# Sixteen sequences of attention and coupling on one core: the coupling's last half added inside the next attention, exp's table loaded behind the last gelu, VectorE's twists behind its maxima, and the side stages on other beats

## The reference

```
left = layernorm(x)[..., :128]                  # attention, 16 heads of 8
q, k, v = left @ Wq.T, left @ Wk.T, left @ Wv.T
att = softmax(q k^T / 4);   y = (att v) @ Wo.T + bo
x = x + layernorm(y)

out = layernorm(x)                              # coupling, 3 cycles
gf = sigmoid(gelu-net of the mean over tokens)
for _ in range(3):
    tf = sigmoid(gelu(gelu(gelu(out @ w1 + b1) @ w2 + b2) @ w3 + b3) @ w4 + b4)
    out = out + (0.1 + 2 * range * (0.7*gf + 0.3*tf - 0.5)) * twist(out)
x = x + layernorm(out)
```

## Time and profile before

| what | value |
|---|---|
| time, median of 3 runs | 3841.51 us (3839.16 to 3843.34) |
| the profiled execution's own time | 3838.75 us |
| its span, first to last instruction | 3836.9 us |
| mean granted TensorE clock | 0.951 of full |
| busy: PE, DVE, ACT, POOL | 92%, 79%, 78%, 24% of the span |
| a full iteration, first exp to first exp | 229.7 to 231.9 us |

### The profile page before, as it was taken

The page is one execution under the profiler, slowest core; times in us unless marked ns, Lnnn a source line. Parts: engine busy times, 40 slices in busy tenths (PEclk is TensorE's granted clock), DMA queues, the critical chain, the costliest instruction groups (busy, mean ns, idle before and its releaser), DMA issues.

```text
span 3836.9 us, 56226 instructions
## 1 busy us (share of the span) xinstructions
PE 3521.5 (92%) x20096; PEld 1037.1 (27%) x20096; DVE 3022.6 (79%) x5740; ACT 2989.7 (78%) x4014; POOL 904.9 (24%) x1258
## 2 busy tenths in 40 slices
PE   3998999999999999989999999999999999999996
PEld 1222232323223232232322223232232322323232
DVE  3997879788797887879788797887879788797832
ACT  2766969788796978869788796878869788796975
POOL 3002040411405023050311404023050320404033
PEclk7997999999999999999999999999999999999998
DMA  3201112021211202112021211202112021111011
GB/s 66 37 21 38 31 30 28 22 49 21 47 22 34 42 16 52 27 41 28 14 55 23 45 23 34 41 17 49 30 41 28 12 55 25 31 26 34 2 34 22
DMA packets 48405, 123.69 MB, mean 32 GB/s; under 512 B 13568, under 2 KB 14976, under 8 KB 40064
## 3 DMA queue, kind: packets, MB, share of 16 engines
q1 hardware_dynamic: 44960, 101.74, 13.3%
q0 software_dynamic: 2304, 16.78, 2.4%
q10 hardware_dynamic: 864, 1.57, 0.3%
HBM read 34.61 MB, written 33.55 MB: 18 GB/s over the span
## 4 chain that ended last, share of the span: by engine, by line
PE 66%; ACT 11%; DVE 9%; POOL 7%; issue 5%; DMA 1%; SPq 0%; ACTq 0%; POOLq 0%; DVEq 0%
PE heads_ps L416 22%; PE ring_ps L378 13%; PE scoresT_ps L401 9%; DVE max_parts L819 8%; PE scoresT_ps L514 7%; ACT p_sb L603 3%; PE scoresT_ps L519 3%; ACT x_in L616 2%; PE scoresT_ps L525 2%; POOL rstd L977 2%; PE scoresT_ps L522 2%; PE ring_ps L445 2%; ACT headsT L612 1%; ACT y_sb L616 1%; POOL rest L998 1%
## 5 line engine op out<-in xcount | busy, mean ns | idle before, releaser
L819 DVE TENSOR_REDUCE max_parts<-ring_ps 128x1 f32<-128x512 f32 x3782 | 2399.7, 684 | 331.9 <-PE ring_ps L378 280.6
L603 ACT ACTIVATE p_sb<-scoresT_ps 128x1024 f32<-128x1024 f32 x2048 | 1985.2, 1023 | 215.1 <-PE scoresT_ps L401 187.0
L378 PE MATMUL ring_ps<-k_rows,q_rows 48*128 48x512 bf16 x3782 | 1111.1, 391 | 73.2 <-DVE max_parts L819 63.4
L416 PE MATMUL heads_ps<-p_sb,v_sb 128*9 128x512 f32 x8192 | 1090.8, 605 | 16.9 <-ACT headsT L612 11.7
L401 PE MATMUL scoresT_ps<-q_rows,k_rows 51*128 51x512 bf16 x4096 | 1040.5, 389 | 44.8 <-ACT p_sb L603 31.3
L378 PEld LDWEIGHTS ring_ps<-k_rows,q_rows 48*128 48x128 bf16 x3782 | 274.6, 94 | 1328.0 <-DVE max_parts L819 1137.1
L969 POOL CAST max_split<-max_all 128x16 bf16<-128x16 f32 x128 | 25.3, 198 | 2117.2 <-DVE max_all L825 2117.2
L514 PE MATMUL scoresT_ps<-state,w 128*128 128x512 f32 x768 | 401.2, 648 | 0.0
L717 ACT ACTIVATE p_sb<-scoresT_ps,b 128x512 f32<-128x512 f32 x192 | 131.5, 685 | 212.7 <-PE scoresT_ps L514 212.5
L401 PEld LDWEIGHTS scoresT_ps<-q_rows,k_rows 51*128 51x128 bf16 x4096 | 219.1, 94 | 263.0 <-ACT p_sb L603 206.6
L416 PEld LDWEIGHTS heads_ps<-p_sb,v_sb 128*9 128x9 f32 x8192 | 123.7, 88 | 328.2 <-issue 280.0
(11 more groups left out here) (171 smaller groups left out, 2870.0 us busy)
## 6 DMA issues: line engine op xcount, KB each, us to landing
q_rows<-parts SPq DMA_DIRECT2D x186, 128.0 KB
k_rows<-parts SPq DMA_DIRECT2D x186, 128.0 KB
x_sb<-in_x SPq DMA_DIRECT2D x16, 1024.0 KB, 4.8
out<-x_sb SPq DMA_DIRECT2D x16, 1024.0 KB, 3.9
out<-x_in POOLq DMA_DIRECT2D x16, 1024.0 KB, 7.9
x_in<-in_x SPq DMA_DIRECT2D x15, 1024.0 KB, 6.4
q_rows<-neg_rows SPq DMA_DIRECT2D x512, 3.0 KB
x_in<-in_x SPq DMA_DIRECT2D x4, 256.0 KB, 3.8
```

The source lines that it names most:

```text
L378: e.matmul(ring_bank(max_taken, u + 1), q_rows[rows, slot, pair, h * BANK + qb * P:h * BANK + (qb + 1) * P], k_rows[rows, slot, pair, kh * ...
L416: m = e.matmul(heads_ps[32 * j:32 * j + DH + 1, :], v_sb[:, b % 2, kb, 4 * (group % NG) + j, 0:DH + 1], p_sb[:, n % 2, j, :], start=(kb == ...
L603: e.activation(p_sb[:, n % 2, 2 * two:2 * two + 2, :].rearrange("p h n -> p (h n)"), scoresT_ps[:, 2 * two * BANK:(2 * two + 2) * BANK], A ...
L819: e.tensor_reduce(max_parts[:, gi % 2, kh, col:col + 1], bank_of(max_taken, u + 1), AX.X, ALU.max).then_inc(max_taken, 1)
```

## The change

Four things are changed.

1. The last twist and update of the third cycle (`c = 1`) leave the end of the beats. They run in the next attention, on VectorE and POOL, behind the units of steps 2 and 5. ACT's affine step for them (`scale_coupling`) moves behind the second exponential of step 0.
2. The first scores of an attention wait for one layer fewer (the second pair waits for the last tanh), and behind the last gelu ACT takes the exponential of one column (`warm`), for which the table is loaded there.
3. On VectorE a beat's twists and updates stand behind that beat's statistics and maxima, no longer ahead of them. Some are a beat earlier.
4. Most of the side stages are on other beats.

```diff
-STATS0, NORM0, TURN_X = (0, 1, 2, 3), (5, 5, 6, 6), (8, 9)
-PROJECT_QK, SPLIT, PROJECT_V, FIRST_ROWS = (13, 14, 15, 16), (14, 15, 16, 19), (19, 20), 22
-BACK, STATS3, NORM3, ADD_OUT = (8, 9, 10, 11), (9, 10, 11, 12), (14, 15, 16, 17), 19
-HEADS1, TURN_TOK, WO, STATS1 = (2, 3, 4, 5), (2, 6), (3, 4, 7, 8), (4, 5, 8, 9)
-NORM1, ADD1, STATS2 = (17, 18, 19, 20), (18, 19, 20, 21), (19, 20, 21, 22)
-NORM2, STATE = (23, 24, 25, 26), (25, 26, 27, 28)
-ROOT0, ROOT1, ROOT2, ROOT3 = 4, 13, 23, 13
+LAST_TWIST, LAST_UPDATE = 2, 5
+STATS0, ROOT0, NORM0, TURN_X = (0, 1, 2, 3), 4, (5, 6, 7, 8), (8, 9)
+PROJECT_QK, SPLIT, PROJECT_V = (17, 18, 23, 24), (19, 20, 25, 26), (20, 26)
+FIRST_ROWS = SPLIT[3]
+BACK, STATS3, ROOT3, NORM3, ADD_OUT = (10, 11, 12, 13), (11, 12, 13, 14), 15, (17, 18, 19, 25), 27
+HEADS1, TURN_TOK, WO, STATS1, ROOT1 = (1, 2, 3, 4), (2, 5), (3, 4, 6, 7), (4, 5, 7, 8), 9
+NORM1, ADD1, STATS2, ROOT2 = (11, 12, 13, 14), (12, 13, 14, 15), (14, 16, 17, 18), 18
+NORM2, STATE = (21, 22, 23, 24), (24, 25, 26, 27)
-TWIST0, UPDATE0, TWIST1, UPDATE1 = 6, 8, 11, 11
+TWIST0, UPDATE0, TWIST1, UPDATE1 = 6, 7, 10, 10
...
 # TensorE, scores
-                if n == 0 and two == 0 and valid(b - 2):
-                    e.wait_ge(hid_done, BEATS * (b - 1))
+                if n == 0 and valid(b - 2):
+                    e.wait_ge(hid_done, BEATS * (b - 1) - (1, 0)[two])
...
 # ScalarE
+            def scale_coupling(b, cycle, l):
+                c = LAYERS[l][1]
+                e.wait_ge(hid_done, layer_end(b, cycle, l))
+                if cycle == 0 and c == 0:
+                    e.wait_ge(shift_ready, b + 1)
+                e.activation(couple[:, c, :], couple[:, c, :], ACT.Identity, bias=shift[:, 0:1],
+                             scale=ar_token[:, 0:1]).then_inc(coupled, 1)
...
                     e.activation(couple[:, c, :], ps, ACT.Tanh, bias=b4_half[:, 0:1],
                                  scale=0.5).then_inc(hid_done, 1)
-                    e.wait_ge(hid_done, layer_end(b, cycle, l))
...
+                    if (cycle, c) != (2, 1):
+                        scale_coupling(b, cycle, l)
...
                         if valid(b):
                             exp(b, n, two)
+                        if valid(b - 2) and (n, two) == (0, 1):
+                            scale_coupling(b - 2, 2, CYCLE - 1)
...
                         layer_out(b - 1, cycle, beat)
+                    if valid(b - 1) and valid(b + 1) and j == LAST_GELU:
+                        e.activation(warm[:, :], ar[:, :], ACT.Exp)
...
 # VectorE and GpSimd, behind the units of step n
+                    if valid(b - 2) and n == LAST_TWIST:
+                        twist(b - 2, 2, 1)
+                    if valid(b - 2) and n == LAST_UPDATE:
+                        update(b - 2, 2, 1)
...
-                if valid(b - 1):
-                    twist(b - 1, 2, 1)
-                    update(b - 1, 2, 1)
```

## The result

| | before | changed |
|---|---|---|
| time, median of 4 runs each on one chip | 3842.3 us | 3677.18 us (3672.35 to 3679.24) |
| span of the profiled execution | 3836.9 us | 3676.5 us |
| granted clock, mean | 0.951 | 0.973 |

The ratio is 0.957, with a 95% interval of 0.9553 to 0.9586: 165 us less. The forecast was 3720 us, 122 less, with 3690 as the low end of its range. The two profiled executions took 3838.75 and 3678.55 us, 160 apart.

The account below looks back on a forecast made before the run. PE, busy 92%, was taken as the bound, losing time to waits and a 1.2 GHz clock. -9.1 us per iteration makes -109 over twelve, -122 with the ends: 3720 us. Range 3690 to 3790; main case 3690 to 3750.

Parts of the forecast that it names:

- The jam and the clock: Beats ahead of attention: separating the two ROOTs removes 4.3 us of PE idle, and the 1.2 GHz stretch behind it, 4.6.
- the rival that the clock still falls: Beats: short waits near beat 23 still drop the clock, the 4.6 us stays, about 3775 us, up to 3795; 25%.
- the 7.7 us that I had worked out for the tables: Beats, per iteration: stages on other beats give -4.3, -0.7 (last layernorm wait), -4.6 (clock) and +1.9 (new waits).
- 1.9 us of new waits: Beats 23 to 28: layer 1 of beat 23 0.6 late, layer 3 of beat 28 0.9 late, margin 0.4.
- -9.1 forecast: Per full iteration: beats -9.3, attention -0.2, 0.4 kept back; twelve make -109 us.
- The hand-over: End of beats: first exponential 1.2 us after layer 4 instead of about 2.8, -1.6; attention, with the last half inside, -0.2.
- the 0.4 that I kept back: Per full iteration: 0.4 us of the gain withheld for what could not be seen.
- The ends: Outside the twelve full iterations: iteration 1 -3, 14 -4, 0 -5, 15 -2, last take_back +1, first attention 0.
- I book 0: VectorE's twists behind maxima: booked 0, since the following update waits for POOL's longer twist anyway.
- The "+3" of that passage: Twists behind maxima: without the cover of POOL's longer twist, 6 delays of at most 0.5 us would add +3.
- the ideal case: Full iterations: no new waits and half of ACT's first-step losses gone, 28 us lower, about 3692; 6%.
- the rival "Slower": PE falls to 1.2 GHz at beat 23 until the attention: +6 or more per iteration, about 3910 us; 3%.

Follow-up runs that it names:

- m2: The changed kernel with the old tables of beat numbers put back; 3817.65 us, 140 us more than the changed kernel.
- p1: The kernel before with the new tables of beat numbers only; 3734.49 us, 107.5 us less than the kernel before.
- x2: The changed kernel with about 5.5 us of idle work on POOL ahead of beat 16's twist, in the twelve full iterations; 3736.82 us.
- p4: The kernel before with only ROOT1 moved, from beat 13 to beat 11; 3816.53 us, ratio 0.9936 to the kernel before.
- m4: The changed kernel with its old end of the coupling (table load, affine step, last twist and update, scores' wait); 3717.62 us.
- m6: The changed kernel with VectorE's twists and updates ahead of the maxima again, the numbers 6, 7, 10, 10 kept; 3696.26 us.
- m5: The changed kernel with the old numbers 6, 8, 11, 11 on both engines, VectorE's twists still behind the maxima; 3785.69 us.
- p2_handover: The kernel before with table load, affine step and last twist and update moved and first scores earlier; 3804.93 us, ratio 0.9909.
- p3_twists: The kernel before with VectorE's twists and updates behind their beat's maxima and the new numbers for them; 3855.29 us, ratio 1.0038.
- m3_twists_back: The changed kernel with VectorE's twists and updates ahead of the maxima and the old numbers 6, 8, 11, 11; 3715.33 us.

## Why the prediction was right in kind and too small

**The jam and the clock.** The step "the two `ROOT`s come apart, so the 4.3 us go, and with the idle cluster the fall of the clock goes" came true, and the rival that the clock still falls did not. m2 and p1 show that the tables do it, and x2 shows the link from wait to clock by making one. But p4 shows that the reason I gave was too narrow: the ROOTs apart save 25.5 us of 107.5, and VectorE's twist then still waits 2.87 us for ACT.

**That p1 lost just the 7.7 us that I had worked out for the tables is partly luck.** My walk used POOL's new order and booked 0.6 at beat 23; p1 has the old numbers and waits 1.45 there. What made it even was PE's wait of 0.78 us for `WO` in the kernel before, which also went and which I had not booked.

**What came in their place.** I booked 1.9 us of new waits. The trace has 0.55, 0.35 and 0.54 with two of 0.21 between them, 1.86 in all, but at other places: 0.35 and not 0.6 at beat 23, 0.21 of the 0.9 at layer 3 of beat 28, and 0.55 (for a bank) and 0.54 (ahead of the last layer 4) that I had not named.

**The failed step is the size of the sum per iteration**, -9.1 forecast, -11.3 - 0.6 = -11.9 measured. It fails in four terms, all on the same side. PE's idle time fell by 8.17 - 3.00 = 5.17 us, of which 1.55 belongs to the hand-over by m4; the other 3.6 stand against 4.3 + 0.7 - 1.9 = 3.1 (0.5). PE's busy time in the beats fell by 84.01 - 77.88 = 6.13 us, of which 0.59 belongs to the hand-over by m4; the other 5.5 stand against 4.6 for the clock (0.9). The hand-over, taken out of the changed kernel, is worth 2.15 in the beats and 0.56 in the attention, against 1.6 and 0.2 (0.9). And the 0.4 that I kept back was not needed. Together 2.7 of the 2.85 us, which make 34 us over twelve iterations. The ends below brought 17.5 us in place of 13, and the medians differ by 5 us more than the profiled executions do. Of the 5.5 us of busy time the 10.54 us at 1.2 GHz explain 4.8, by half of PE's busy share in them; the remaining 0.7 I have not settled.

**Twists behind maxima.** "I book 0" was wrong as a price of the part. Taken back it costs 38 us, 3.2 per iteration, and its halves taken back cost 19 (m6) and 108 (m5). The "+3" of that passage is per iteration, for VectorE's twist coming late without the cover of POOL's longer one; no run takes away that cover alone. The walk had looked at VectorE alone. What it missed is that the numbers also move POOL's twist ahead of a `split_low` and its update ahead of a transfer's issue. About 1 us of the 2.9 was in the walk already, since it counted POOL's rows in the new order. The part depends on the tables: alone it loses 13 us, and the three parts alone add to 107.5 + 37 - 13 = 131.5 of the 165.

**The hand-over.** The order was as written (0.57 us from tanh to exponential against 0.7). I had counted only the time to the first exponential, and not PE's first scores. With the old end, as m4_handover_back has it, PE waits for them:

```profile
1203.47 0.39 PE L400 MATMUL scoresT_ps<-q_rows,k_rows 51*128 51x512 bf16 x2 [0.82 <-DMA q_rows<-neg_rows]
```

The row names a DMA, but `scores` waits for the last layer result too, and these matmuls start 0.10 us behind the end of the last tanh (1202.68 to 1203.37), as in the kernel before (1248.97, then 1249.07). In the changed kernel the first pair of scores needs one layer result less, this wait isn't there, and the work of PE that it held up lies ahead of the first exponential. Of the load the Trainium skill ("ScalarE: Activation LUTs", *What ACT_TABLE_LOAD costs*) has 2.66 us per switch, load and drain. The trace doesn't agree here: each of the 29 loads of the changed kernel that stand between two activations takes 1.28 us, 0.02 behind the activation ahead of it and 0.01 ahead of the next one. Taking the early load out costs 1.6 per hand-over, which is nearer to the row.

**The ends.** Iteration 0 was forecast at -5 and brought 9.5 us (63.1 to 53.6), all of it by the tables, as p1's 52.6 shows. Iteration 1 brought 5.4 against 3, iteration 14 3.3 against 4. The time to the first attention rose by 1.6 where I had 0, and the stretch behind the last attention fell by 0.9 against 1. Both are no larger than what kernels with no edit there show: p2_handover and p3_twists reach the first attention 1.4 and 1.6 us sooner than the kernel before, and x2_pool_late has 2.8 us more behind the last one than the changed kernel. So these two say nothing on the terms.

**The range.** Its low end was the ideal case taken from the sum, 28 us below it. The terms that I had marked as uncertain were those of new waits, which came out as booked (1.86 against 1.9); the removed ones, the hand-over and the part booked at 0 had no bounds on the side on which they failed. Its high end is off too: 3720 + 23 + 6 x 2.2 is 3756, not 3750. And in the rival "Slower" the 4.6 us of the clock are counted twice, since they are in the 9.1 already: 20 - 9.1 is +10.9 per iteration, about 3970 us, and it decides from 9.1 us of lost clock on, not 13.7.

## What to carry to other kernels

When a table places work on several in-order engines, walk every engine's queue for each number that changes, not only the engine whose wait one has in mind: here one beat on POOL was worth 1.1 us of PE's wait, twelve times, and as much again at the attention's start. Price an edit both alone and inside the full change, since p3 alone says +13 and the same part taken out of the changed kernel says +38. And where a wait of PE stands ahead of a stretch at half clock, count both: in x2 a further 2.8 us of idle time made the beats 5.0 us longer.

## What the runs showed of the hardware

**Two-input products on VectorE and GpSimd hold each other up.** The product of 128x512 takes POOL 1.27 us alone and 1.72 to 1.77 beside VectorE's, and VectorE's update takes 0.69 alone and 2.35 beside POOL's of 1.55. 2.35 is 0.69 + 1.55 and 0.1 more, so VectorE's did not share but waited. In the changed kernel 130 of POOL's twists and updates run alone or start ahead of VectorE's and take 1.26 to 1.28 us, and the 62 that start behind it take 1.71 to 1.80; VectorE's take 0.66 to 0.69 alone or first, and up to 1.61 when they start behind. The Trainium skill says this in "SBUF — State Buffer" (*SBUF: two separate sides*): the pair of ports that both use is held for the whole instruction by the one that starts first, and the other blocks. The changed kernel's rows agree. The row of 2.35 us agrees that one of them waits, but not on which: VectorE's starts 0.24 us ahead of POOL's and is the one that waits. POOL's issue of the transfer, 1204.94 to 1205.88, overlaps its start; whether that is the reason no run shows. POOL's mean twist is 1634 ns in the kernel before, 1524 in m3_twists_back and 1381 in the changed kernel, where VectorE's comes later.

**The clock falls behind much shorter waits than the jam's, and not every time behind the same ones.** In m5_numbers_back it stands at 1.2 GHz for 3.4 us from about the end of the wait of 1.65 us on, in all twelve full iterations. Behind the wait of 2.41 us it does so in six of them and stays at full clock in the other six. In m6_order_back waits of 0.44, 0.21 and 1.12 us within 3.5 us stand in all twelve. Ahead of sequence 5 the clock stays at 1.00 behind them:

```profile
1179.00:1189.20 10.20, 8.68 (x28) 3.66 (x29) 8.61 (x23) 7.95 (x16) 7.10 (x8) 1.00 0.16 66
```

and ahead of sequence 4 (and of 13) it falls:

```profile
953.61 0.39 PE L381 MATMUL ring_ps<-k_rows,q_rows 48*128 48x512 bf16 x1 [0.44 <-DVE max_parts L833]
954.21 0.39 PE L381 MATMUL ring_ps<-k_rows,q_rows 48*128 48x512 bf16 x1 [0.21 <-DVE max_parts L833]
...
956.72 1.19 PE L434 MATMUL scoresT_ps<-feat_x,wq 128*128 128x512 f32 x1 [1.12 <-DVE max_parts L833]
```

```profile
956.20:966.40 10.20, 9.69 (x18) 4.27 (x19) 6.23 (x19) 6.38 (x12) 6.15 (x9) 0.50 0.01 2
```

These beats take 87.4 us in place of 82.7. So one iteration can't tell whether a cluster of short waits costs the clock; all twelve have to be read.
